# A PSUM copy on another engine, a GELU in two operations, and a reordered last sequence in a transformer block kernel

## The reference

```
xn  = layernorm(x)
out = x + attention(xn) + experts(xn)
attention: q, k, v = split(xn @ Wqkv + b)       # 16 heads of 8
           f(q), f(k) = exp(clip(normalised q, k @ omega - node, -20, 20))   # 64 features a head
           causal linear attention: sum f(q).f(k) v / sum f(q).f(k), then @ Wout + bout
experts:   logits = rms_norm(xn) @ rms_norm(slots).T     # 512 slots
           slot inputs = softmax over tokens' share of xn, normalised
           h = gelu(slot inputs @ w1);  processed = h @ w2      # 128 -> 512 -> 128
           out = processed mixed by a softmax over the 512 slots
```

## Time and profile before

| what | value |
|---|---|
| median of three runs | 446.14 us (445.23 to 446.38) |
| the profiled execution | 445.07 us, its span 443.3 us |
| PE, PEld busy | 431.2 us (97%), 361.1 us (81%) |
| DVE, ACT, POOL busy | 347.5 us (78%), 320.0 us (72%), 186.3 us (42%) |
| chain that ended last | PE 93%, DVE 4%, ACT 2% |

### The profile page before, as it was taken

The page is one execution under the profiler, slowest core; times in us unless marked ns, Lnnn a source line. Parts: engine busy times, 40 slices in busy tenths (PEclk is TensorE's granted clock), DMA queues, the critical chain, the costliest instruction groups (busy, mean ns, idle before and its releaser), DMA issues.

```text
span 443.3 us, 15786 instructions
## 1 busy us (share of the span) xinstructions
PE 431.2 (97%) x5726; PEld 361.1 (81%) x5726; DVE 347.5 (78%) x872; ACT 320.0 (72%) x533; POOL 186.3 (42%) x278
## 2 busy tenths in 40 slices
PE   6889999999999999999999999999999999999896
PEld 3568888888888889888888988888898888889785
DVE  7898777978878797878869787796978779576653
ACT  4767786858768686786868678586876859677681
POOL 5424444543435444343643443464345345434320
PEclk9999999999999999999999999999999999999999
DMA  4400321030202003020110302011030200203001
GB/s 93 107 25 3 62 49 27 1 63 14 53 20 47 18 6 59 12 47 24 37 23 12 59 12 47 24 22 37 12 59 12 47 12 9 51 1 61 2 1 25
DMA packets 45323, 14.37 MB, mean 32 GB/s; under 512 B 35376, under 2 KB 45168, under 8 KB 45296
## 3 DMA queue, kind: packets, MB, share of 16 engines
q1 hardware_dynamic: 44448, 13.48, 14.8%
q10 hardware_dynamic: 720, 0.53, 0.4%
q0 software_dynamic: 128, 0.01, 0.1%
HBM read 3.44 MB, written 2.10 MB: 12 GB/s over the span
## 4 chain that ended last, share of the span: by engine, by line
PE 93%; DVE 4%; ACT 2%; issue 1%; DVEq 0%; ACTq 0%
PE x L1070 20%; PE p_s L1120 10%; PE p_t L1120 8%; PE x L1271 7%; PE x L1238 7%; PE x L1280 6%; PE x L1292 6%; PE x L1133 5%; PE p_s L1133 5%; PE x L1211 4%; PE p_s L1105 2%; PE x L1222 2%; PE x L1246 2%; PE x L1187 2%; PE p_t L1105 2%; PE x L1175 1%
## 5 line engine op out<-in xcount | busy, mean ns | idle before, releaser
L488 POOL TENSOR_TENSOR s_sb<-s_sb,causal 128x256 f32<-128x256 f32 x96 | 68.3, 731 | 79.5 <-ACT s_sb L584 79.5
L578 ACT ACTIVATE feat<-arg,f_bias 128x1024 f32<-128x1024 f32 x64 | 71.8, 1147 | 8.4 <-DVE arg L848 8.3
L848 DVE TENSOR_SCALAR arg<-p_s,f_low,f_high 128x1024 f32<-128x1024 f32 x32 | 42.9, 1340 | 18.7 <-PE p_s L1105 12.2
L1120 PEld LDWEIGHTS p_s<-feat 64*64 64x64 f32 x1024 | 38.8, 132 | 17.2 <-issue 15.5
L1120 PE MATMUL p_s<-feat 64*64 64x256 f32 (+3 forms) x1024 | 49.5, 309 | 1.3 <-ACT feat L578 1.3
L329 POOL TENSOR_TENSOR qk_sq<-qkv 128x512 f32<-128x512 f32 x15 | 15.6, 1040 | 82.9 <-DVE qkv L825 82.9
L482 POOL TENSOR_TENSOR s_sb<-s_sb,causal 128x512 f32<-128x512 f32 x30 | 37.6, 1276 | 26.0 <-ACT s_sb L590 26.0
L1120 PE MATMUL p_t<-feat 64*64 64x256 f32 (+3 forms) x1024 | 47.1, 299 | 0.3 <-issue 0.3
L1120 PEld LDWEIGHTS p_t<-feat 64*64 64x64 f32 x1024 | 41.3, 133 | 1.8 <-issue 0.4
L848 DVE TENSOR_SCALAR arg<-p_t,f_low,f_high 128x1024 f32<-128x1024 f32 x32 | 42.7, 1335 | 0.0
L1238 PEld LDWEIGHTS x<-xg,disp 128*128 128x128 f32 x256 | 29.9, 191 | 8.2 <-ACT disp L606 8.2
(11 more groups left out here) (165 smaller groups left out, 1035.4 us busy)
## 6 DMA issues: line engine op xcount, KB each, us to landing
xin<-in_L_attn_x_dram SPq DMA_DIRECT2D x31, 64.0 KB, 2.3
out_dram<-out_sb SPq DMA_DIRECT2D x31, 64.0 KB, 2.1
se_rows<-n_L_ffn_slot_embeds_dram SPq DMA_DIRECT2D x2, 128.0 KB, 4.4
w_f<-in_L_ffn_w_dram SPq DMA_DIRECT2D x1, 256.0 KB, 4.0
w_sb<-in_L_ffn_w_dram SPq DMA_DIRECT2D x1, 256.0 KB, 4.0
stack_t<-stack SPq DMA_TRANSPOSE x16, 4.3
wqkv_f<-in_L_attn_Wqkv_dram ACTq DMA_DIRECT2D x1, 192.0 KB, 4.1
bqkv_bc<-in_L_attn_bqkv_dram ACTq DMA_DIRECT2D x1, 192.0 KB, 4.8
```

The source lines that it names most:

```text
L488: pool.tensor_tensor(v, v, m, ALU.mult).then_inc(mb_ok, 1)
L578: nc.scalar.activation(feat[:, k:k + 2, :], arg[:, k:k + 2, :], ACT.Exp, bias=f_bias[:, 0:1]).then_inc(fe_ok, 1)
L848: nc.vector.tensor_scalar(arg[:, k:k + 2, :], (p_s, p_t)[g % 2][:, :, :], f_low[:, 0:1], f_high[:, 0:1], ALU.max, ALU.min).then_inc(cl_ok, 1)
L1120: mm = nc.tensor.matmul(dst[rows:rows + 64, u, o:o + hi - lo], f[:, T + keys:T + keys + 64], f[:, lo:hi], start=True, stop=True, skip_grou ...
```

## The change

Five edits, all of order or of engine; the arithmetic is the same, except that sums of three products are added in another order.

1. The low copy leaves ScalarE for VectorE (`low_copy`), between `bn_stats` and the rest of `ln_stats`, which is split in two functions for it. It is in sequences 1 to 15; the copy that ends the program stays on ScalarE.
2. The GELU of half 0 becomes two operations, of bank 1 and then of bank 0. `hidden` fills bank 1 first, and `processed_low` takes chunk m = 1 first and the chunks that overwrite bank 1 (c = 2, 3) before the others, with a wait at each pair of matmuls.
3. In `hidden`, the product with the low part `slot_lo` comes third, and alone waits for it.
4. In sequence 15 VectorE clips `p_s` and `p_t` one after the other before `slots_norm`, and ScalarE does both exponentials of features, the high context copy and the two evacuations before `slots_high`.
5. In sequence 15 TensorE turns the slots between `scores(1)` and `scores(2)`, not ahead of `scores(0)`.

```
-            def gelu(b, half):
-                after(act, hd_ok, count(b, 2, half + 1))
-                nc.scalar.activation(hid_t[:, 2 * half:2 * half + 2, :], (x01, x23)[half][:, :, :],
-                                     ACT.Gelu).then_inc(ge_ok, 1)
+            def gelu_low(b):
+                after(act, hd_ok, count(b, 2, 1))
+                for m in (1, 0):
+                    nc.scalar.activation(hid_t[:, m, :], x01[:, m, :], ACT.Gelu).then_inc(ge_ok, 1)
...
# ScalarE, row
                 evac_pair(bp, 6)
                 evac_pair(bp, 7)
-                ctx_copy(bp, 0)
                 dispatch_exp(b)
                 combine_exp(b)
                 feature_exp(b, 0)
...
+                else:
+                    feature_exp(b, 1)
                     ctx_copy(bp, 1)
+                    evac_b(b, 0)
+                    evac_b(b, 1)
+                    slots_high(b)
...
# VectorE
+            def low_copy(b):
+                after(dve, cx_ok, count(b, 4, 2))
+                after(dve, ct_ok, count(b, 1, 0))
+                nc.vector.tensor_copy(ctx_sb[:, 0, :].rearrange("p (j t) -> p j t", j=TILES),
+                                      home(b, 0)).then_inc(cs_ok, 1)
...
                 if nxt2:
+                    ln_gather(b2)
+                low_copy(bp)
+                if nxt2:
                     ln_stats(b2)
                 clip(b, 0)
+                if not nxt:
+                    clip(b, 1)
                 slots_norm(b, 0)
                 slots_norm(b, 1)
-                clip(b, 1)
-                if nxt:
+                if nxt:
+                    clip(b, 1)
                     qkv_bias(b1)
...
# TensorE, hidden
-                for m in (2 * half, 2 * half + 1):
+                for m in ((1, 0), (2, 3))[half]:
...
+                    nc.tensor.matmul(dst, w1_hi[:, sl], slot_hi[:, :], start=True, stop=False, skip_group_check=True)
+                    nc.tensor.matmul(dst, w1_lo[:, sl], slot_hi[:, :], start=False, stop=False, skip_group_check=True)
+                    if m == 1:
+                        after(pe, sll_ok, count(b, 1, 1))
...
# TensorE, processed_low
                 for m in parts:
-                    for c in range(NCH):
+                    for c in (2, 3, 0, 1):
+                        if c % 2 == 0:
+                            after(pe, ge_ok, count(b, 3, 1 if m == 1 and c == 2 else 2))
...
# TensorE, row
-                slots_transposed(b)
+                if nxt:
+                    slots_transposed(b)
                 scores(b, 0)
                 scores(b, 1)
                 if nxt:
                     lump_high(bp, False)
+                else:
+                    slots_transposed(b)
```

More of the change, by code:

```diff
@@ L614, in slots_high, with gelu_high @@
                 nc.scalar.activation(slot_hi[:, :], x01[:, 0, :], ACT.Copy).then_inc(slh_ok, 1)
-            def gelu(b, half):
-                after(act, hd_ok, count(b, 2, half + 1))
-                nc.scalar.activation(hid_t[:, 2 * half:2 * half + 2, :], (x01, x23)[half][:, :, :],
-                                     ACT.Gelu).then_inc(ge_ok, 1)
+            def gelu_low(b):
+                after(act, hd_ok, count(b, 2, 1))
+                for m in (1, 0):
+                    nc.scalar.activation(hid_t[:, m, :], x01[:, m, :], ACT.Gelu).then_inc(ge_ok, 1)
+            def gelu_high(b):
+                after(act, hd_ok, count(b, 2, 2))
+                nc.scalar.activation(hid_t[:, 2:4, :], x23[:, :, :], ACT.Gelu).then_inc(ge_ok, 1)
             def proc_copy(b, h):
@@ L692, in first_row @@
                 nc.scalar.preload_act_table_set(GELU)
-                gelu(b, 0)
+                gelu_low(b)
                 evac_b(b, 2)
                 evac_b(b, 3)
-                gelu(b, 1)
+                gelu_high(b)
                 nc.scalar.preload_act_table_set(LN_EXP)
@@ L722, in row @@
                     ln_root(b2)
-                if not nxt:
-                    ctx_copy(bp, 1)
-                slots_high(b)
-                evac_b(b, 0)
-                feature_exp(b, 1)
-                evac_b(b, 1)
-                if nxt:
+                if nxt:
[3 more added lines that the diff above has]
+                    evac_b(b, 1)
+                    ctx_copy(bp, 1)
+                else:
+                    feature_exp(b, 1)
                     ctx_copy(bp, 1)
+                    evac_b(b, 0)
+                    evac_b(b, 1)
+                    slots_high(b)
                 evac_b(b, 2)
@@ L781, in newton, with ln_gather @@
                 after(dve, done, count(base, 3, extra))
-            def ln_stats(b):
+            def ln_gather(b):
                 after(dve, d_x[b[1]], landed(b, 1))
@@ L787, in ln_stats @@
                 last.then_inc(ln_s, 1)
+            def ln_stats(b):
                 hold(dve, ln_s, count(b, 3, 1))
@@ L928, in _ @@
             nc.vector.memset(vw[:, :, :, :, :], 0.0).then_inc(vz_const, 1)
+            ln_gather(b0)
             ln_stats(b0)
@@ L976, in first_row @@
                 slot_maxima(b)
+                ln_gather(b1)
                 ln_stats(b1)
@@ L1170, in ctx_transposed @@
                 else:
-                    after(pe, ge_ok, count(b, 2, 4))
+                    after(pe, ge_ok, count(b, 3, 6))
                 for g in range(2):
@@ L1250, in hidden @@
                 if half == 0:
-                    after(pe, sll_ok, count(b, 1, 1))
                     after(pe, slh_ok, count(b, 1, 1))
@@ L1261, in hidden @@
                     sl = slice(128 * m, 128 * m + 128)
-                    mm = three((x01, x23)[half][:, m % 2, :], w1_hi[:, sl], w1_lo[:, sl], slot_hi[:, :],
-                               slot_lo[:, :], True, True)
+                    dst = (x01, x23)[half][:, m % 2, :]
+                    nc.tensor.matmul(dst, w1_hi[:, sl], slot_hi[:, :], start=True, stop=False, skip_group_check=True)
+                    nc.tensor.matmul(dst, w1_lo[:, sl], slot_hi[:, :], start=False, stop=False, skip_group_check=True)
+                    if m == 1:
+                        after(pe, sll_ok, count(b, 1, 1))
+                    mm = nc.tensor.matmul(dst, w1_hi[:, sl], slot_lo[:, :], start=False, stop=True,
+                                          skip_group_check=True)
                 mm.then_inc(hd_ok, 1)
             def processed_low(b, parts):
-                after(pe, ge_ok, count(b, 2, 1))
                 for m in parts:
-                    for c in range(NCH):
+                    for c in (2, 3, 0, 1):
+                        if c % 2 == 0:
+                            after(pe, ge_ok, count(b, 3, 1 if m == 1 and c == 2 else 2))
                         o = 128 * (c % 2)
                         nc.tensor.matmul(x01[:, c // 2, o:o + 128], hid_t[:, m, 128 * c:128 * c + 128],
-                                         w2_sb[:, m, :], start=(m == 0 and c % 2 == 0), stop=False,
+                                         w2_sb[:, m, :], start=(m == 1 and c % 2 == 0), stop=False,
                                          skip_group_check=True)
             def processed_high(b):
-                after(pe, ge_ok, count(b, 2, 2))
+                after(pe, ge_ok, count(b, 3, 3))
                 for c in range(NCH):
@@ L1345, in first_row @@
                 scores(b, 3)
-                processed_low(b, (0,))
+                processed_low(b, (1,))
                 project(b, 2)
                 project(b, 3)
-                processed_low(b, (1,))
+                processed_low(b, (0,))
                 processed_high(b)
@@ L1385, in row @@
                 project(b, 3)
-                processed_low(b, (0, 1))
+                processed_low(b, (1, 0))
                 ctx_transposed(bp)
```

1 line of the change is left out of this document (added).

## The result

The changed kernel took 442.77 us (median of four runs, 442.58 to 443.55), the kernel before beside it 445.98 us (445.23 to 446.38). The ratio is 0.9944, with a 95% interval of 0.9931 to 0.9957: faster by 1.9 to 3.1 us. The four runs of before stood high: in the later comparisons its median over 35, 23 and 9 runs was 445.23, 445.37 and 445.25. The sum was made on the profiled execution, and there the comparison is 445.07 us before and 442.89 now, 2.18 us less; the sum said 2.0.

A forecast was written before the change was run, and what follows sets the result against it. TensorE's instruction stream was taken as the bound; 0.36 (low copy) + 0 + 0 + 0.30 (sequence 0) + 1.34 (sequence 15) = 2.0 us off the median of 446.14 gave 444.1 us, range 443.1 to 445.7.

The forecast's parts named there:

- The sum: Whole kernel: 0.36 + 0 + 0 + 0.30 + 1.34 = 2.0 us saved, made against the profiled execution of 445.07 us.
- TensorE's stream is the bound: Whole kernel: TensorE is busy 26.10 of 26.10 us a sequence, so other engines' edits return only its real waits.
- Low copy, 0.36 us: Loop, before `slot_sums`: moving the copy off ScalarE saves 0.06 us in each of six even sequences.
- Equal idle times of different causes: Before `processed_low`: loads idle 0.42 us in the loop and in sequence 15, so splitting the GELU gains 0.
- Sequence 0, 0.30 us: Sequence 0: waiting for `slot_lo` only at the third product saves 0.26 + 0.10 - 0.06 us, set by ScalarE's chain.
- Sequence 15, 1.34 us: Sequence 15: an earlier second clip and exponential and later turned slots start `scores(2)` at 419.15 instead of 420.49.
- 0.2 us to spare: Sequence 15: margin by which `slots_low` should end before the third product of `hidden` needs it; the tightest place.
- 0.1 us a sequence in the loop: Rival: new work costs TensorE 0.1 us in each of 13 sequences, 1.3 us, giving 445.4; chance 0.14.
- Copy locked out: Rival: GpSimd's mask delays VectorE's low copy 0.59 us and the projection with it, 4.5 us slower, 450.6; chance 0.07.
- Sequence 15 gives less than half: Rival: `slots_low` or an evacuation replaces the exponential as the wait in sequence 15; gain 1.3 us, 444.9; chance 0.10.
- More waits go in the loop: Rival: split GELU and earlier `disp` each give 0.1 us a sequence, 2.6 us on top of 1.64, 441.9; chance 0.07.

The follow-up runs named there:

- e2_gelu: Kernel before with only the GELU of half 0 split in two, bank 1 first; `hidden` still waits for `slot_lo` first: 445.54 us, ratio 1.0009.
- e10_nosplit: Changed kernel with the first GELU half in one operation again, all else as changed: 442.75 us, ratio 0.9942 against the kernel before.
- e4_last: Kernel before with only sequence 15's new order (clips and exponentials first, slots turned between scores); `slot_lo` waited for ahead of all products: 444.10 us, ratio 0.9980.
- e5_lowfirst: Changed kernel, but `hidden` waits for `slot_lo` ahead of its first product again: 443.72 us, ratio 0.9953 against the kernel before.
- e6_noturn: Changed kernel, but TensorE turns the slots ahead of `scores(0)` again in sequence 15: 443.78 us, ratio 0.9953 against the kernel before.
- e8_lock: Changed kernel plus an unused SBUF-to-SBUF copy on VectorE ahead of the low copy in sequences 1 to 15: 447.10 us, ratio 1.0031 against the kernel before.
- e11_psum: Changed kernel plus an unused copy of 128x256 fp32 from PSUM on VectorE ahead of the low copy: 443.50 us, ratio 0.9957 against the kernel before.
- e9_loop: Changed kernel with the order of sequence 15 used in every later sequence of the loop too: 443.21 us, ratio 0.9950 against the kernel before.
- e3_lowlast: Kernel before with `hidden` filling bank 1 first and waiting for `slot_lo` only at its third product, GELU in one operation: 445.08 us, ratio 0.9993.

## Why the prediction was right, point by point

- **TensorE's stream is the bound, and only its real waits can be given back.** Right, as far as it was tried: VectorE's 6.3 us more of work in the loop cost nothing.
- **Low copy, 0.36 us.** Right: 0.37 in the changed kernel, 0.35 with the edit alone, and only in even sequences (0.04 to 0.10 in each of the six in the loop). The copy takes 0.42 us, where 0.41 was taken. L802 was held until `residual` ended and the clip wasn't missed, as said.
- **Equal idle times of different causes (0.42 us before `processed_low`) aren't waits.** Right, shown twice (e2_gelu, e10_nosplit).
- **Sequence 0, 0.30 us.** The mechanism was right (ScalarE's chain sets the gain), the term too small: 0.46. "0.26 us of idle time, plus some 0.1 us by which back-to-back operations overlap, less 0.06" left out that there are two evacuations, and that the second can overlap too. Before, it started 0.54 us behind the first, when its scores were ready; now 0.37 behind it, with the same overlap of 0.10. The first gained 0.34, the second 0.17 more, and the GELU took 0.04 back. Without the split GELU the stretch is another 0.06 shorter.
- **Sequence 15, 1.34 us.** Right: 1.34, measured from the start of sequence 15 to the end. That the hundredths agree is luck: counted from the same start, `scores(2)` comes 1.38 us earlier and `hidden` 1.41, and 0.06 of it is lost again in the last transfer, whose issue lies 2.80 us ahead of the end of the span before and 2.86 now. "0.2 us to spare" for `slots_low` was 0.16, and without edit 3 the time is 0.18 (e4_last) to 0.22 us (e5_lowfirst) longer. What I had not seen is that the turned slots also cover an evacuation; that is worth 0.28 us (e6_noturn).
- **Rivals.** *0.1 us a sequence in the loop*: not there. *Copy locked out*: not there, and over-priced: it would have delayed the copy by 0.59 us, e8_lock delayed it by 0.58, and that run stands at 447.1, not 450.6. The step that failed in it is "and the projection with it": the projection had 0.2 to 0.3 us of room. *Sequence 15 gives less than half*: no. *More waits go in the loop*: no. The Trainium skill's rule on the shared ports (SBUF — State Buffer, section "Who interferes with whom") is borne out by the pair e8_lock and e11_psum: SBUF source held until GpSimd's operation ends, PSUM source not.
- **From the sum to the median.** This is where the time left the range. The sum and the profiled executions agree to 0.2 us, but I set the forecast 1 us above the sum, at a median of three runs of 446.14; 67 later runs of the same kernel have medians of 445.2 to 445.4. The median of few runs was the weaker anchor, and 445.07, the profiled run, the better one: less 2.0 it gives 443.1. The measured change of the median, 1.9 to 3.1 us by its interval, holds both the 2.0 of the sum and the 2.18 of the profiles.

## What to carry to other kernels

Find who is late in each stretch, and compare an idle time with the same place where the suspected cause is missing, before calling it a wait. Where steps stand in a fixed order, a move can need its partner: edit 5 without edit 4 lost 1.1 us in sequence 15, edit 4 without edit 5 gained 0.8 there, and both together 1.3. Where GpSimd is at work, keep on VectorE what reads PSUM, and look for operations that work from SBUF (here a copy of 0.67 us, a `tensor_scalar` of 0.61) in front of anything that TensorE needs.

## What the runs showed that I had not expected

- **Which of two operations comes first can cost half a microsecond.** In the profiled run of e9_loop, sequence 0 starts 0.87 us later than in the changed kernel, in a part of the program that is the same. GpSimd's first `residual` and VectorE's product `qk_sq` run beside each other in both, but in another order. The changed kernel:

```profile
11.94 0.69 DVE L329 TENSOR_TENSOR qk_sq<-qkv 128x512 f32<-128x512 f32 x1
12.04 1.18 POOL L463 TENSOR_TENSOR xres<-xin,bout_bc 128x256 f32<-128x256 f32 x1 [4.92 <-DMA bout_bc<-in_L_attn_bout_dram]
```

and e9_loop:

```profile
12.23 0.73 POOL L463 TENSOR_TENSOR xres<-xin,bout_bc 128x256 f32<-128x256 f32 x1 [5.11 <-DMA bout_bc<-in_L_attn_bout_dram]
12.28 1.22 DVE L329 TENSOR_TENSOR qk_sq<-qkv 128x512 f32<-128x512 f32 x1
```

  Whichever engine comes first, the other takes some 0.5 us longer. Of the 0.87 us, 0.34 are there when `qk_sq` starts, and 0.53 are its own longer run, which the changed kernel left to GpSimd: `residual`, held by its transfer, is only 0.19 us later, and so comes first. The 0.34 us come from TensorE. The matmuls of zeros with which it begins start 0.64 us apart and from some moment on 0.32. That moment is the one from which the trace records the full granted clock (the 2.4 GHz level): 6.26 us in the changed kernel, 7.28 in e9_loop, where the transposes behind these matmuls start at 7.66 instead of 7.26 and ScalarE's copy of their result 0.34 us later. In eleven of the thirteen traces the moment lies between 4.51 and 6.56 us, and sequence 0 starts at 14.62 to 14.64; in e3_lowlast it is 7.06 and 14.87, in e9_loop 7.28 and 15.51. This execution of e9_loop took 444.01 us, the lowest of the five 443.16.
- **The transposing transfer varies.** In e5_lowfirst one of 16 took 6.1 us from issue to landing, where the middle one takes 4.3, and TensorE stood 1.30 us for it. These are seen once or twice each; how much of the scatter of 1 to 2 us between runs of one kernel is theirs wasn't shown. It can't be all: of the 67 later executions of before, the spans lie between 443.1 and 444.7 us, and what the time has beyond the span goes from 1.7 to 2.7 us by itself.
